# A graph network kernel: two more dense destination blocks in the third pass, their weights built behind pass one

## What is computed

```python
def gcn_layer(x, row, col, w, W, b, n):
    x = x @ W
    deg = jax.ops.segment_sum(w, col, num_segments=n)
    dinv = jnp.where(deg > 0, jax.lax.rsqrt(deg), 0)
    norm = dinv[row] * w * dinv[col]
    out = jax.ops.segment_sum(norm[:, None] * x[row], col, num_segments=n)
    return out + b

x = _layernorm(x + L0(x))                 # attention over the first edges
x = _layernorm(x + L1(x))                 # pass 1: unit edge weights
h = relu(gcn_layer(x, row, col, w, W1, b1, n))     # pass 2
h = relu(gcn_layer(h, row, col, w, W2, b2, n))     # pass 3
x = _layernorm(x + h)
x = _layernorm(x + L3(x))                 # dense over all blocks, at the end
```

## Time and profile before

| | |
|---|---|
| runs | 3383.58, 3397.59, 3399.66 us; median 3397.59 |
| span of the profiled execution | 3382.6 us |
| pass 1 | 232 to 1412 us: 882 chunks, 49 blocks built, 20 of them weighed |
| pass 2 | first chunk 1429.2, last 2128.4 us: 522 chunks, 980 units |
| pass 3 | first chunk 2149.2, last 2825.8 us: 522 chunks, 980 units |
| last stage | 2873 to 3382 us |

### The profile page before, as it was taken

One profiled execution on the slowest core, in us unless ns is written; L12 is line 12 of the kernel. 1 busy time (PEld: TensorE's weight loads), 2 busy tenths in 40 slices (PEclk: granted clock), 3 DMA queues, 4 the chain that ended last, 5 costly groups with the idle time before them and its releaser, 6 DMA issues.

```text
span 3382.6 us, 57833 instructions
## 1 busy us (share of the span) xinstructions
PE 3130.2 (93%) x18133; PEld 2496.3 (74%) x18133; DVE 2316.4 (68%) x9106; ACT 1705.3 (50%) x4513; POOL 2071.9 (61%) x2051
## 2 busy tenths in 40 slices
PE   6789999999999998899999999899999997999999
PEld 5666676766776776678888887677777775888887
DVE  6657998988998998577777777466666664233323
ACT  3555676676677676444444444344444443232332
POOL 6627777777777777677777777577777772000000
PEclk9889999999999999999999999899999998999999
DMA  6256787777787787666666665766666666344443
GB/s 198 75 179 194 227 256 229 248 241 234 233 258 237 243 258 220 226 194 206 200 201 207 200 194 174 255 201 201 196 205 199 195 188 223 137 148 161 165 165 115
DMA packets 331236, 683.89 MB, mean 202 GB/s; under 512 B 62964, under 2 KB 180176, under 8 KB 330030
## 3 DMA queue, kind: packets, MB, share of 16 engines
q1 hardware_dynamic: 231374, 411.18, 35.6%
q0 software_dynamic: 97616, 267.10, 27.6%
q10 hardware_dynamic: 1936, 1.84, 0.2%
HBM read 495.63 MB, written 184.26 MB: 201 GB/s over the span
## 4 chain that ended last, share of the span: by engine, by line
PE 54%; DMA 18%; DVE 16%; POOL 5%; ACT 4%; issue 3%; SPq 0%; DVEq 0%; ACTq 0%
DMA G<-T,idx 15%; PE PS L1996 14%; PE PS L1924 11%; PE PS L1965 7%; PE PS L1967 3%; PE PS L1888 3%; POOL G L2059 3%; DVE soh L1372 3%; DVE R L1272 2%; PE PS L1855 2%; PE PS L1754 2%; PE PS L1864 2%; PE PS L1755 2%; PE PS L1876 2%; DVE M L1263 2%
## 5 line engine op out<-in xcount | busy, mean ns | idle before, releaser
L2059 POOL DMA_INDIRECT G<-T,idx x1926 | 1952.4, 1014 | 644.6 <-issue 278.1
L1924 PE MATMUL PS<-H,aw 128*128 128x256 f32 x3920 | 1018.6, 382 | 0.3 <-DMA aw<-AW 0.3
L1609 ACT ACTIVATE R<-G,wD 128x256 fp32r<-128x256 f32 x1044 | 522.7, 507 | 733.9 <-DMA G<-T,idx 494.6
L1924 PEld LDWEIGHTS PS<-H,aw 128*128 128x128 f32 x3920 | 736.0, 191 | 104.2 <-DMA aw<-AW 0.7
L1272 DVE SCALAR_TENSOR_TENSOR R<-G,wD,R 128x256 fp32r<-128x256 f32 x1044 | 506.7, 485 | 420.8 <-ACT R L1609 415.3
L1965 PE MATMUL PS<-G,M 128*128 128x257 f32 x1764 | 576.1, 410 | 91.1 <-DMA G<-T,idx 31.1
L1967 PE MATMUL PS<-R,Mr 128*128 128x512 f32 x1044 | 600.0, 576 | 47.2 <-DVE R L1272 44.1
L1996 PE MATMUL PS<-HH,cr 128*128 128x512 f32 x2205 | 501.2, 390 | 0.3 <-DVE cr L1450 0.3
L1996 PEld LDWEIGHTS PS<-HH,cr 128*128 128x128 f32 x2205 | 413.4, 188 | 87.9 <-DVE cr L1450 2.4
L1652 ACT CAST atp<-PS 128x512 bf16<-128x512 f32 x588 | 336.5, 572 | 208.6 <-PE PS L1876 202.0
L1965 PEld LDWEIGHTS PS<-G,M 128*128 128x128 f32 x1764 | 293.2, 198 | 179.4 <-DVE soh L1372 31.7
(11 more groups left out here) (231 smaller groups left out, 3857.3 us busy)
## 6 DMA issues: line engine op xcount, KB each, us to landing
aw<-AW SPq DMA_DIRECT2D x280, 448.0 KB, 3.6
AT<-atp SPq DMA_DIRECT2D x539, 128.0 KB
br<-AT SPq DMA_DIRECT2D x77, 896.0 KB, 4.7
AW<-awp SPq DMA_DIRECT2D x240, 256.0 KB
G<-T,idx POOLq DMA_INDIRECT x1926
AT<-atf SPq DMA_DIRECT2D x49, 256.0 KB
T<-H SPq DMA_DIRECT2D x96, 128.0 KB
cr<-AT SPq DMA_DIRECT2D x7, 1024.0 KB, 4.7
```

Of the source, the lines that this page charges most:

```text
L1609: e.activation(R[m % NR][:, 0:D], G[slot][:, 0:D], ACT.Copy, scale=wD[:, k // NC, k % NC:k % NC + 1]).then_inc(s_rw, 1)
L1924: ins = e.matmul(ps, aw[n_ % NAW][:, s_ % 7, :], H[:, s_, :], start=s_ == 0, stop=s_ == NBK - 1)
L2059: e.indirect_dma_start(G[slot][:, 0:D], None, TAB[p][0:N, :], bass.IndirectOffsetOnAxis(ap=idx[:, k // NC, k % NC:k % NC + 1], axis=0)).th ...
```

## The change

The number of dense blocks becomes a number for each pass: 20 in pass 2 as before, 22 in pass 3. Pass 3 has 27 x 18 = 486 chunks in place of 522, and 22 x 49 = 1078 units in place of 980. The 22 largest blocks (`NDW`, `NBW` = 27) are weighed behind pass 1, in place of 20. Pass 2 reads the last 20 of the 22 slabs. Semaphore counts follow (`DN0`, `MOFF`). `SLACK`, `LEAD` and the rings keep their sizes; a filler tile of SBUF gets smaller by what `payw` and `wrest` grow.

```diff
-ND = 20
-NB0 = NBK - ND
+ND = {2: 20, 3: 22}
+NB0 = {p: NBK - n for p, n in ND.items()}
+DN0 = {2: 0, 3: ND[2] * 7, 4: (ND[2] + ND[3]) * 7}
+NDW = max(ND.values())
+NBW = NBK - NDW
...
-FILL_B, FILL_C = 1208, 380
+FILL_B, FILL_C = 1208, 290
...
-    return NK if p == 1 else NB0 * NC
+    return NK if p == 1 else NB0[p] * NC
...
-def dense_of(k):
+def dense_of(p, k):
 
-    return min(ND * NBK, LEAD + k * (ND * NBK - LEAD) // (chunks_of(2) - SLACK))
+    return min(ND[p] * NBK, LEAD + k * (ND[p] * NBK - LEAD) // (chunks_of(p) - SLACK))
...
-    dense = {(2 * d + 1) * NBK // (2 * ND): NB0 + d for d in range(ND)}
-    others = iter(range(NB0))
+    dense = {(2 * d + 1) * NBK // (2 * NDW): NBW + d for d in range(NDW)}
+    others = iter(range(NBW))
...
-                if b >= NB0:
+                if b >= NBW:
                     S_.append((at_ + 1, ("third", i, j // CB)))
...
-            if b >= NB0:
+            if b >= NBW:
                 T_.append((at_ + 2, ("weigh", i, j)))
...
-                    AW[n_ // 7, :, (n_ % 7) * 7 * P:(n_ % 7 + 1) * 7 * P], s_la[i % NAW])
+                    AW[NB0[p] - NBW + n_ // 7, :, (n_ % 7) * 7 * P:(n_ % 7 + 1) * 7 * P], s_la[i % NAW])
...
-                return [(free(max(0, 7 * (n_ - NAW + 1))), (load, p, n_)) for n_ in range(ND * 7)]
+                return [(free(max(0, 7 * (n_ - NAW + 1))), (load, p, n_)) for n_ in range(ND[p] * 7)]
```

More of the change, by code:

```diff
@@ L214, in complete @@
     for i in range(NBK - chunks_of(p) // NC):
-        done.append((min(k for k in range(chunks_of(p) + 1) if dense_of(k) >= NBK * (i + 1)), NB0 + i))
+        done.append((min(k for k in range(chunks_of(p) + 1) if dense_of(p, k) >= NBK * (i + 1)), NB0[p] + i))
     return sorted(done)
@@ L227, in follow_pass @@
     for k, b in complete(p):
-        rest = ("rest",) if b < NB0 else ("none",)
+        rest = ("rest",) if p > 1 and b < NB0[p] else ("none",)
         if p > 1:
@@ L325, in head_steps @@
     end = chunks_of(3)
-    k0 = min(k for k in range(end) if dense_of(k) >= ND * NBK) + 2
+    k0 = min(k for k in range(end) if dense_of(3, k) >= ND[3] * NBK) + 2
     there = {b: d + 1 for d, (kind, b) in FOLLOW[3][1] if kind == "table"}
@@ L849, in weighed_before @@
         def weighed_before(i):
-            return sum(b >= NB0 for b in BORDER[:i])
+            return sum(b >= NBW for b in BORDER[:i])
         def fills():
             return [(kind, i, m_) for i, b in enumerate(BORDER) for m_ in range(NSG)
-                    for kind in (("keep", "keepw") if b >= NB0 else ("keep",))]
+                    for kind in (("keep", "keepw") if b >= NBW else ("keep",))]
         FILLS = fills()
@@ L881, in built @@
             for i in range(3):
-                w.wait_ge(s_wp[i], 16 * len(range(i, ND * NSG, 3)))
+                w.wait_ge(s_wp[i], 16 * len(range(i, NDW * NSG, 3)))
             w.wait_ge(s_pc, NPOS * NBK)
-            w.wait_ge(s_wg, NPOS * ND)
+            w.wait_ge(s_wg, NPOS * NDW)
             w.wait_ge(s_v, at["bad"])
@@ L1235, in follow @@
                 elif kind == "sum" and p == 3:
-                    after(("rest", 3, b) if b < NB0 else ("bias", b))
+                    after(("rest", 3, b) if b < NB0[3] else ("bias", b))
                     done(e.scalar_tensor_tensor(out=X[:, b, :], in0=hbi, scalar=0.0, in1=X[:, b, :],
@@ L1349, in behind_ @@
                                               OH[j][:, :, :].unsqueeze(1).to_broadcast([P, n_, NPOS, NC]))
-                    if b >= NB0:
+                    if b >= NBW:
                         after("piece2")
-                        done(e.tensor_tensor(OHP[:, 2:5, :, :], *spread_(payw[:, b - NB0, :, :], 3), ALU.mult))
+                        done(e.tensor_tensor(OHP[:, 2:5, :, :], *spread_(payw[:, b - NBW, :, :], 3), ALU.mult))
                     done(e.tensor_tensor(OHP[:, 0:2, :, :], *spread_(pay2[:, b, :, :], 2), ALU.mult), ("load", i))
@@ L1367, in behind_ @@
                         w.wait_ge(s_pc, batch_end(before))
-                        if BORDER[before // NBT] >= NB0:
+                        if BORDER[before // NBT] >= NBW:
                             w.wait_ge(s_wg, batch_end(before) - NPOS * (before // NBT - weighed_before(before // NBT)))
@@ L1561, in follow @@
                 if kind == "relu":
-                    w.wait_ge(s_v, at["rest", 2, b] if b < NB0 else at["sum", 2, b])
+                    w.wait_ge(s_v, at["rest", 2, b] if b < NB0[2] else at["sum", 2, b])
                     hbi = hb[PLACE[2][b] % 3][:, :]
@@ L1623, in behind_ @@
                     i = step[1]
-                    q_ = 5 if BORDER[i] >= NB0 else 2
+                    q_ = 5 if BORDER[i] >= NBW else 2
                     w.wait_ge(s_pm, NC * (i + 1))
@@ L1860, in behind_ @@
                     c = step[2]
-                    q_ = 5 if b >= NB0 else 2
+                    q_ = 5 if b >= NBW else 2
                     w.wait_ge(s_v, max(at["place", i, c], at["load", i]))
@@ L1917, in unit @@
                     elif p == 3:
-                        w.wait_ge(s_v, at["sum", 2, NB0 + ND - 2 + (d - ND) % 2])
+                        w.wait_ge(s_v, at["sum", 2, NBK - 2 + (d - ND[2]) % 2])
                     else:
                         w.wait_ge(s_ar, NBK * NSG)
-                        w.wait_ge(s_kw, ND * NSG)
+                        w.wait_ge(s_kw, NDW * NSG)
                 rows_there(w, p, s_)
@@ L1950, in aggregate @@
                     if p > 1:
-                        for u in range(dense_of(k - 1) if k else AHEAD, dense_of(k)):
+                        for u in range(dense_of(p, k - 1) if k else AHEAD, dense_of(p, k)):
                             unit(p, u)
@@ L2131, in loads @@
             def loads(p):
-                free = lambda u: min(k for k in range(chunks_of(p) + 1) if dense_of(k) >= u)
-                return [(free(max(0, 7 * (n_ - NAW + 1))), (load, p, n_)) for n_ in range(ND * 7)]
+                free = lambda u: min(k for k in range(chunks_of(p) + 1) if dense_of(p, k) >= u)
+                return [(free(max(0, 7 * (n_ - NAW + 1))), (load, p, n_)) for n_ in range(ND[p] * 7)]
             def stores(p):
@@ L2215, in settled @@
         def settled():
-            return [(s_v, at["all"]), (s_ev, project_at(4, NBK)), (s_nm, 3 * NBK - len(SHARED)), (s_ng, len(SHARED)), (s_mm, MOFF[4]), (s_dn, 2 * ND * 7),
+            return [(s_v, at["all"]), (s_ev, project_at(4, NBK)), (s_nm, 3 * NBK - len(SHARED)), (s_ng, len(SHARED)), (s_mm, MOFF[4]), (s_dn, DN0[4]),
                     (s_xt, turn_at(4, NBK)), (s_tb[1], 16 * NBK), (s_tb[2], 16 * NBK), (s_t3[0], 16 * ((NBK + 1) // 2)),
```

34 lines of the change are left out of this document (17 added, 17 removed).

## The result

The changed kernel took 3355.7 us in the median of four executions, beside 3395.6 us for the kernel before; the ratio is 0.9891 with a 95% interval of 0.9873 to 0.9909. So the change makes the kernel 1.1% faster: 37 and 38 us by the two ratios, 40 and 31 us by the two pairs of medians. The forecast was 3384 us, 13.6 us less than before, in a range of 3366 to 3408 us. It had the sign, the mechanism (TensorE takes over as the bound of pass 3) and somewhat over a third of the size, and the measured time lies outside its range.

The account below looks back on a forecast made before the run. Gathering was taken to pace pass 3, with TensorE becoming its bound after the change. Pass 3 17.5 us less and pass 1 3.9 us more made -13.6 us, from 3397.6 to 3384 us, range 3366 to 3408 us.

Parts of the forecast that it names:

- What bounds the kernel: Pass 3: paced by gathering at 1.286 us a chunk; with the change TensorE's work, 1.317 us, becomes the bound.
- The middle part: Pass 3 from first chunk to last with units: TensorE 98% filled, 621 us in place of 638.4, 17.5 us less.
- the price of the degrees: Pass 2: TensorE's work for a group of degrees, taken as 0.70 us.
- Rival (a): Pass 3: TensorE without gaps, part with units 608 us, 3372 us in all; chance 0.16.
- rival (b): Pass 3: gathering still sets the pace, part with units 594 us, 3357 us in all; chance 0.05.
- The tail: Pass 3's last 24 chunks, behind the units: taken as unchanged at 38 us.
- Pass 1: Two more weighed blocks behind pass 1, at 1.9 us more than a plain block each: 3.9 us more.
- Rival (d): Pass 1: weighed blocks cost TensorE's full time, +24 us in place of +4, 3404 us in all; chance 0.18.
- The prediction's estimate after the Trainium skill: Pass 1: if each of 26 added VectorE operations held a gather up for its full length, 10.8 us more.
- Rival (c): Pass 3: TensorE's idle time is strict-order latency and stays, 1.447 us a chunk, 35 us slower, 3432 us; chance 0.09.
- The sum: Whole kernel: 3.9 - 17.5 = -13.6 us, put on the median 3397.6 us, giving 3384 us.

Follow-up runs that it names:

- e6: Kernel before with 21 dense blocks in pass 3 in place of 20, and 21 weighed; 3369.4 us, ratio 0.9939 to before.
- e4: Changed kernel with 24 dense blocks in pass 3 in place of 22, and 24 weighed; 3389.4 us, ratio 1.0008 to before.
- e7: Changed kernel with pass 3's units ending 12 chunks before its end, not 24, and the last stage's heads moved closer; 3352.2 us, ratio 0.9891 to before.
- e8: Changed kernel with 21 dense blocks in pass 2 too, in place of 20; 3360.3 us, ratio 0.9905 to before.
- e1: The kernel before, run again with no edit for a second trace; 3389.5 us.
- e2: Changed kernel with pass 3 back at 20 dense blocks, 22 still weighed; 3391.1 us, ratio 1.0007 to before.
- e3: Changed kernel with only 20 blocks weighed, 22 dense in pass 3, values not the reference's; 3362.4 us, ratio 0.9907 to before.
- e10: Changed kernel with 28 blocks weighed behind pass 1 in place of 22; 3385.4 us in one execution.

## Why the prediction was wrong in size

**What bounds the kernel, right.** Pass 3 was paced by gathering at 1.286 us a chunk and is now paced by TensorE. e6 (1.291 a chunk, gathers pace), the change (1.32) and e4 (645.5 / 426 = 1.515) stand on the slower of the two lines. Next to the crossing, in e7, 0.5% was lost.

**The middle part, mis-sized.** "I take 98%: 1.317 / 0.98 = 1.344 us, 621 us" is the term that failed first. The work a chunk, 1.317, was right: 462 x 1.317 = 608 against 611.6 and 611.1 measured, and 2 to 3 us of the rest are lost in the first 50 us of the pass. The fill was not: from 2210 to 2770 us the prices leave 0.7 of 560 us, 99.9%, and no start was late. I had taken pass 2, 97.5% filled, as the nearest row, and had written beside it that its gathers were at 1.34 us, their own limit there, and then gave that only half a per cent. Two resources that are both nearly full cannot tell by themselves which of them leaves the other idle. Of the 2.5%, 0.7 were the price of the degrees, too low (e8); the rest was left by the gathers: pass 2's time follows their issue length, and with less gathering and more TensorE work (e8) the idle time is gone. Rival (a) had the right mechanism, at 3372 us. That the measured 3355.7 us lies at the 3357 of rival (b) is luck: by (b) the middle part takes 594 us, and it took 611. This term: -29.3 us measured (the mean of three traces with 20 dense blocks, 640.7, to the mean of the change's two, 611.35), -17.5 forecast. 2.3 of the difference are that the first trace of before lay below the mean.

**The tail, a term set to nothing.** "I take them as the 38 us that they were" failed. The tail's instructions are the same, but its start is not: when TensorE is the bound, gathers run ahead, and the tail starts with 9 of its 24 out instead of 4. -5.9 us (38.5 to 32.6), and ScalarE's waits for gathered rows in it fall by as much, from 6.5 us in the mean of the three traces to 0.6. e6 agrees, where gathers still pace: 5 out, 36.9 us. That a stage with the same instructions starts from another filling of its buffers was not looked for. In e4, with 9 out, it is 32.7. In pass 2, where 6 to 7 were out before already, e8's 9 gave nothing.

**To the last stage**: 46.6 us in the mean of before, e1 and e2, 44.7 in the change's two traces, -1.9. e6 had 50.5. Why it is 44.3 to 44.8 in each run with TensorE as pace (but for e7, which moved the heads) and scattered elsewhere is open.

**Pass 1, held.** 3.9 us forecast; e2 has +2 (-3 to +8), which is also room for nothing at all, and between 10 and 28 blocks it is 2.9 us a block in the mean, unevenly spread. Rival (d), 24 us, is excluded. That the traces of 22 weighed blocks (1180.8 to 1189.8) and of 20 (1179.7 to 1188.6) do not differ shows only that they scatter by more than the effect. The prediction's estimate after the Trainium skill, SBUF — State Buffer, section Who interferes with whom (10.8 us), is above e2's interval: if the added operations held gathers up, it was by less than their full length.

**Rival (c), excluded**: idle time that the engine pays in its strict order would have stayed in the change, e4 and e3, where there is none in the steady stretch; e7 shows 0.5%, and the rival needed 10%.

**The sum.** -29.3 - 5.9 - 1.9 + about 3 in pass 1 (an estimate between e2's 2 and the forecast's 3.9) is -34 us, beside -37 and -38 us by the ratios of the two comparisons, whose intervals (6 and 8 us to either side) hold it; for e3, without the 3, it is -37 beside -32 (12 to either side). The 40 us between the first two medians hold some 8 us of chance in four executions of before. The forecast put its difference on a median of three, 3397.6 us, some 10 us above the 3387 us of the later comparisons; from there the same -13.6 would have read 3374 us, 18 us above the measured time.

## What to carry to other kernels

When two resources pace one loop, work out both lines (here TensorE's 0.43 a unit + 0.23 a chunk + 1.10 a block, and 1.286 a gather) and take the slower one without a discount, unless a stretch in which only one of them is near its limit shows a loss. Idle time of an engine in a loop that another resource paces said nothing here of how full it can be. And a stage behind the changed one is not free because its instructions are the same: ask how many buffers are filled when it starts.

## What the runs showed of the hardware

TensorE ran for 560 us without a gap, at a granted clock of 1.00, on operands that ScalarE and VectorE wrote just in time into a ring of three; I had expected a per cent or two of lost time in so tight a hand-over, and there was at most 0.1%. Issuing a gather of 128 rows took 0.94 us at the least, with at least 0.30 us between two of them, in every pass; the mean length went from 967 ns (e4, pass 3) to 1039 ns (e10, pass 1). The first unit instruction (f32) behind a group of 8 small bf16 matmuls took 0.257 us to the next start in place of 0.216.
